# Pair sums on GpSimd and half-width Hadamard products in the last stage of a four-stage transformer kernel

## The reference, cut to what matters

```python
def act_quant(x, bits=8):
    qb = float(2 ** (bits - 1))
    scale = qb / jnp.clip(jnp.max(jnp.abs(x), axis=-1, keepdims=True), 1e-05)
    return jnp.clip(jnp.round(x * scale), -qb, qb - 1) / scale
def h_bitlinear(x, w):
    return jnp.einsum('bsh,oh->bso', act_quant(fwht(x)), weight_quant(w))
gate = bitlinear(x, w_gate)            # 1024 outputs
up = bitlinear(x, w_up)
x = x + h_bitlinear(jax.nn.silu(gate) * up, w_down)   # x is the layer norm's output inside
```

## Time and profile before

| | |
|---|---|
| median of 3 executions | 580.14 us (578.57 to 585.94) |
| the profiled execution | 581.71 us |
| its span, first to last instruction | 579.9 us |
| busy: TensorE, VectorE, ScalarE, GpSimd | 85%, 78%, 62%, 55% |

### The profile page before, as it was taken

How to read it: one execution, slowest core, us unless ns; L and a number is a source line. 1 busy time by engine, 2 the same in 40 slices (tenths; PEclk the granted TensorE clock), 3 DMA queues, 4 the chain that set the end, 5 groups by cost and what they waited for, 6 DMA issues and landing times.

```text
span 579.9 us, 11051 instructions
## 1 busy us (share of the span) xinstructions
PE 495.6 (85%) x3338; PEld 436.4 (75%) x3338; DVE 450.2 (78%) x1358; ACT 357.8 (62%) x903; POOL 318.6 (55%) x298
## 2 busy tenths in 40 slices
PE   0599979998889898995659999999899999588894
PEld 0478757877788887994449999999799998346673
DVE  4779967875877786756598889999989887769674
ACT  2345547253558676763237877878688889666643
POOL 2547671014467886415767788788577773363100
PEclk9989999999999998996597999999999999989997
DMA  8144454312364555545820000000000000000000
GB/s 276 38 126 129 131 152 126 90 58 67 98 195 111 188 187 161 144 131 145 284 62 19 28 21 19 29 19 1 2 1 2 2 1 2 0 1 9 11 28 27
DMA packets 27961, 45.24 MB, mean 78 GB/s; under 512 B 5697, under 2 KB 18849, under 8 KB 27265
## 3 DMA queue, kind: packets, MB, share of 16 engines
q1 hardware_dynamic: 21056, 28.15, 15.8%
q0 software_dynamic: 3792, 10.74, 7.2%
q10 hardware_dynamic: 3056, 5.65, 3.1%
HBM read 34.63 MB, written 8.85 MB: 75 GB/s over the span
## 4 chain that ended last, share of the span: by engine, by line
PE 48%; DVE 24%; issue 10%; DMA 7%; ACT 6%; POOL 5%; SPq 0%; DVEq 0%; ACTq 0%; POOLq 0%
PE bank L415 8%; PE bank L416 8%; PE bank L417 8%; PE bank L1080 8%; PE bank L1521 5%; DMA bw<-bits_dram 2%; DVE pT_lo L1580 2%; DVE sc L2081 1%; ACT pr L956 1%; PE bank L1476 1%; DVE X L1632 1%; DMA inb<-rows_kept,row_of 1%; DMA seg<-seg_dram 1%; DVE asel L1632 1%; PE bank L1282 1%
## 5 line engine op out<-in xcount | busy, mean ns | idle before, releaser
L584 POOL DMA_INDIRECT inb<-rows_kept,row_of x47 | 47.4, 1008 | 37.8 <-PE bank L1080 20.8
L956 ACT ACTIVATE pr<-sc,smin 128x256 f32<-128x256 f32 x128 | 63.3, 502 | 0.0
L661 POOL TENSOR_TENSOR Q_lo<-Q,Q_hi 128x512 fp32r<-128x512 f32 x32 | 41.5, 1297 | 22.7 <-ACT Q_hi L695 22.1
L2081 DVE CUSTOM_DVE_ANT_0 sc<-bank,bias 128x256 f32<-128x256 f32 x128 | 46.5, 418 | 0.1
L648 POOL TENSOR_TENSOR pr<-pr,srec 128x512 f32<-128x512 f32 x32 | 33.4, 1042 | 21.6 <-DVE srec L2088 21.6
L1580 DVE TENSOR_TENSOR pT_lo<-bank,pT_hi 128x512 fp32r<-128x512 f32 x64 | 41.1, 683 | 5.0 <-ACT pT_hi L695 5.0
L695 ACT ACTIVATE pT_hi<-bank 128x512 fp32r<-128x512 f32 x64 | 35.0, 595 | 13.6 <-PE bank L1080 13.3
L612 POOL DMA_INDIRECT yk<-slots_y,slot x32 | 33.7, 1052 | 14.0 <-issue 5.8
L655 POOL TENSOR_TENSOR Q<-Q,rot 128x512 f32<-128x512 f32 x32 | 41.2, 1286 | 0.0
L1080 PE MATMUL bank<-const,pr 128*128 128x128 f32 x256 | 34.8, 279 | 6.6 <-POOL pr L648 6.5
L965 ACT ACTIVATE pr<-pr,srec 128x256 f32<-128x256 f32 x64 | 29.1, 502 | 16.7 <-DVE srec L2088 16.7
(11 more groups left out here) (346 smaller groups left out, 1939.5 us busy)
## 6 DMA issues: line engine op xcount, KB each, us to landing
slots_y<-yb SPq DMA_DIRECT2D x47, 128.0 KB
wg_raw<-gate_up_dram SPq DMA_DIRECT2D x22, 256.0 KB, 2.8
bw<-bits_dram ACTq DMA_DIRECT2D x3, 1024.0 KB
wd_raw<-down_dram SPq DMA_DIRECT2D x16, 128.0 KB, 2.1
wo<-wo_dram SPq DMA_DIRECT2D x2, 1024.0 KB, 6.7
wd_raw<-down_dram SPq DMA_DIRECT2D x30, 64.0 KB, 2.2
gu_raw<-gate_up_dram SPq DMA_DIRECT2D x6, 256.0 KB, 3.5
X<-x_dram SPq DMA_DIRECT2D x2, 512.0 KB, 6.8
```

The source lines that it names most:

```text
L584: pool.indirect_dma_start(inb[:, j % NIN, :], None, rows_d, bass.IndirectOffsetOnAxis(row_of[:, j:j + 1], 0)).then_inc(slots_in[j % NIN], 16)
L661: pool.tensor_tensor(Q_lo[:, i % 2, :], Q[:, i % 2, :], Q_hi[:, i % 2, :].bitcast(F32), ALU.subtract).then_inc(queries_low_g, 1)
L956: e = act.activation(pr[:, i % 2, z, :], sc[:, i % 2, z, :], ACT.Exp, bias=smin[:, i % 2, z:z + 1], scale=-1.0, accum_out=ssum[:, i % 2, z ...
L2081: dve.tensor_tensor_reduce(sc[:, r, z, :], bank[2 + h][:, u * S:(u + 1) * S], bias[:, TB * b_ + u, :], 1.0, 3.0e38, ALU.add, ALU.min, smin ...
```

## The change

- GpSimd makes of two neighbouring units their sum and their difference (`pair`, tile `sd`), and high and low parts are taken of these, no longer of `hp`. The units' order of feature groups is changed to fit (`chunk`, `part_of`).
- The transform has one Hadamard level less to do: per tile 16 matmuls of 256 columns, each group pair going to its own half of a bank, with two by two signed copies in place of four by four.
- Transforms of tiles 4 and 6 use banks 2 and 3, those of 0 to 3, 5 and 7 banks 4 and 5.
- VectorE does `butterfly(t+1)` before `clip(t)`, and `x4(t-1)` at the end of step `t`. TensorE does `transform(t+1)` ahead of `turn_f(t-1)` from step 3 on.
- `feature_scale` has three small operations in place of four.

```diff
+            def pair(v, op):
+                if v >= 2:
+                    pool.wait_ge(bit_low_g, v - 1)
+                return pool.tensor_tensor(sd[:, v % 2, :], hp[:, 0, :], hp[:, 1, :], op).then_inc(pair_g, 1)
+            def lo_b(v):
+                pool.wait_ge(hidden_high_a, UNITS + v + 1)
+                n = v // NF
+                pool.tensor_tensor(hp_lo[n][:, part_of(v), :], sd[:, v % 2, :], hp_hi[n][:, part_of(v), :].bitcast(F32),
+                                   ALU.subtract).then_inc(bit_low_g, 1)
+            for v in range(0, 2 * NF, 2):
+                if v == BESIDE - 2:
+                    power3(NT - TB, TB)
+                pool.wait_ge(hidden_v, UNITS + v + 2)
+                pair(v, ALU.add)
+                pair(v + 1, ALU.subtract)
+                lo_b(v)
+                lo_b(v + 1)
...
             def hi_b(v):
-                act.wait_ge(hidden_v, UNITS + v + 1)
-                copy(hp_hi[n][:, c, :], hp[:, v % 2, :]).then_inc(hidden_high_a, 1)
+                act.wait_ge(pair_g, v + 1)
+                copy(hp_hi[v // NF][:, part_of(v), :], sd[:, v % 2, :]).then_inc(hidden_high_a, 1)
...
                 silu_b(v)
-                hi_b(v - 1)
+                hi_b(v - 2)
                 if v == LATE_TURN:
                     for t in range(NT - TB, NT):
                         bits_x(t)
+            hi_b(AHEAD - 2)
             hi_b(AHEAD - 1)
             f_copy(0)
...
+                for z in range(2):
+                    if w is not None:
+                        pe.wait_ge((butterfly_v, transform_copied_a)[z], (2 * (w + 1), w + 1)[z])
+                    for k in range(2):
+                        out = bank[transform_bank(t) + z][:, k * D:(k + 1) * D]
+                        for y, part in enumerate((hp_hi[n], hp_lo[n])):
+                            for r in range(2):
+                                e = pe.matmul(out, part[:, 4 * z + 2 * k + r, tile],
+                                              had[:, r, :, :].rearrange("p q j -> p (q j)"),
+                                              start=(y == 0 and r == 0), stop=(y == 1 and r == 1))
...
+            transform(3)
+            for t in range(3, NT + 2):
+                final(t - 2)
+                if t + 1 < NT:
+                    transform(t + 1)
+                if t <= NT:
+                    turn_f(t - 1)
...
                 if v >= 2:
-                    dve.wait_ge(bit_low_g, v - 1)
+                    dve.wait_ge(pair_g, v - v % 2)
                 dve.tensor_tensor(hp[:, v % 2, :], gsl[:, v % 2, :], bank[unit_bank(v, 1)][:, :], ALU.mult
...
+            butterfly(0)
+            for t in range(NT + 1):
                 if t < NT:
                     feature_scale(t)
                 for v in units_after(t):
                     gate_b(v)
+                if t + 1 < NT:
+                    butterfly(t + 1)
                 if t < NT:
                     clip(t)
                 for v in units_after(t):
                     up_b(v)
+                if t >= 1:
+                    x4(t - 1)
```

More of the change, by code:

```diff
@@ L237, in build @@
             m[k] for k in ("q_hi q_lo rot Q Q_hi Q_lo sc pr pT_hi pT_lo o_hi o_lo fqT hn2 sin2").split()]
-        xqT, invB, diag, gt, gsl, hp, had, f1, F = [m[k] for k in "xqT invB diag gt gsl hp had f1 F".split()]
+        xqT, invB, diag, gt, gsl, hp, had, sd, f1, F = [m[k] for k in "xqT invB diag gt gsl hp had sd f1 F".split()]
         hp_hi, hp_lo = [m["hpB_hi"], m["hpA_hi"]], [m["hpB_lo"], m["hpA_lo"]]
@@ L381, in x_bank, with chunk, part_of, transform_bank @@
             return t % 2 if t < NT - TB else 6 + t % 2
+        def chunk(v):
+            z, c0 = divmod(v % NF // 2, 2)
+            return 4 * z + 2 * (v % 2) + c0
+        def part_of(v):
+            z, c0 = divmod(v % NF // 2, 2)
+            return 4 * z + 2 * (v % 2) + c0
+        def transform_bank(t):
+            return 2 if t >= 4 and t % 2 == 0 else 4
+        def last_transform(t):
+            return max((w for w in range(t) if transform_bank(w) == transform_bank(t)), default=None)
         def final_bank(t):
@@ L984, in signs @@
                 act.wait_ge(masked_v, 4 * PAIRS)
-                for r in range(4):
-                    for q in range(4):
-                        e = act.activation(had[:, r, q, :], had1, ACT.Copy, scale=-1.0 if odd(r & q) else 1.0)
-                e.then_inc(signs_a, 1)
+                for r in range(2):
+                    for q in range(2):
+                        act.activation(had[:, r, q, :], had1, ACT.Copy, scale=-1.0 if r and q else 1.0)
             def bits_x(t):
@@ L1036, in f_copy @@
                     act.wait_ge(butterfly_v, 2 * (t - 1))
-                copy(f1[:, t % 2, :], bank[5][:, :]).then_inc(transform_copied_a, 1)
+                copy(f1[:, t % 2, :], bank[transform_bank(t) + 1][:, :]).then_inc(transform_copied_a, 1)
             def f_round(t):
@@ L1512, in transform @@
                 n, x = divmod(t, NT // 2)
-                tile = slice(x * P, (x + 1) * P)
-                for part, ready in ((hp_hi[n], hidden_high_a), (hp_lo[n], bit_low_g)):
-                    pe.wait_ge(ready, (UNITS if ready is hidden_high_a else 0) + NF * (n + 1))
-                    for z in range(2):
-                        if t >= 1 and ready is hidden_high_a:
-                            pe.wait_ge((butterfly_v, transform_copied_a)[z], (2 * t, t)[z])
-                        for r in range(4):
-                            m_ = had[:, r, :, :].rearrange("p q j -> p (q j)")
-                            e = pe.matmul(bank[4 + z][:, :], part[:, 4 * z + r, tile], m_,
-                                          start=(r == 0 and ready is hidden_high_a), stop=(r == 3 and ready is bit_low_g))
-                        if ready is bit_low_g:
-                            e.then_inc(transform_p, 1)
+                tile, w = slice(x * P, (x + 1) * P), last_transform(t)
+                pe.wait_ge(hidden_high_a, UNITS + NF * (n + 1))
+                pe.wait_ge(bit_low_g, NF * (n + 1))
+                if t == 4:
+                    pe.wait_ge(hidden_v, UNITS + 2 * NF)
+                for z in range(2):
[4 more added lines that the diff above has]
+                        for y, part in enumerate((hp_hi[n], hp_lo[n])):
+                            for r in range(2):
+                                e = pe.matmul(out, part[:, 4 * z + 2 * k + r, tile],
+                                              had[:, r, :, :].rearrange("p q j -> p (q j)"),
+                                              start=(y == 0 and r == 0), stop=(y == 1 and r == 1))
+                    e.then_inc(transform_p, 1)
             def turn_f(t):
@@ L1553, in _ @@
                 products(v)
-            pe.wait_ge(signs_a, 1)
             pe.wait_ge(xq_copied_a, 2 * NT)
-            for t in range(NT + 2):
-                if t < NT:
-                    transform(t)
+            for t in range(3):
+                transform(t)
                 if t >= 2:
                     final(t - 2)
-                for v in units_after(t)[:1]:
-                    products(v)
-                if 1 <= t <= NT:
+                products(AHEAD + 2 * t)
+                if t >= 1:
                     turn_f(t - 1)
-                for v in units_after(t)[1:]:
-                    products(v)
+                products(AHEAD + 2 * t + 1)
+            transform(3)
[5 more added lines that the diff above has]
+                    turn_f(t - 1)
         @block.vector
@@ L2253, in _ @@
             up_b(AHEAD - 1)
-            for t in range(NT + 2):
-                if t < NT:
-                    butterfly(t)
-                if t >= 2:
-                    x4(t - 2)
+            butterfly(0)
+            for t in range(NT + 1):
                 if t < NT:
```

28 lines of the change are left out of this document (11 added, 17 removed).

## The result

Four executions of the changed kernel have a median of **605.75 us** (604.54 to 608.4); four of the kernel before beside it 581.49 (578.57 to 585.94). The ratio is 1.040, with an interval from 1.036 to 1.045. The forecast was 608. The profiled execution took 606.64 us, its span 604.7.

A forecast was written before the change was run, and what follows sets the result against it. TensorE was half the chain; late tiles were bound by a 5.98 us loop of transform, copy and butterfly. Terms 9.1 + 15.9 - 0.4 + 3.3 = 27.9 us gave 609.6 profiled, 608 on the median, range 602 to 615.

The forecast's parts named there:

- R0: Start of tile 0's rounding; forecast at 532.6 in place of 523.5, 9.1 us later, with GpSimd setting the pace before the loop.
- R0 to R3: Early tiles, from tile 0's rounding to tile 3's: 37.8 us (11.1 + 11.1 + 15.6) against 21.9, 15.9 more.
- The third step: From tile 2's rounding to tile 3's: 15.6 us, waiting for four GpSimd operations, transform(4), half a turn and bits.
- R3 to R7: Late tiles, tile 3's rounding to tile 7's: four steps of 6.25 us, 25.0 against 25.4, set by VectorE and ScalarE.
- the TensorE loop worked out beforehand: Late tiles: half a turn, bits, final, transform and hand-overs, 4.95 us a tile, shorter than the 6.25 forecast.
- The clock: TensorE at the 1.2 GHz level after longer gaps, mainly at transform(0) and transform(4): 3.3 us added, bounded by 0 and 5.
- The sum: All forecast terms together: 27.9 us more, so the profiled execution would take 609.6 us in place of 581.7.
- the GpSimd operations come onto the chain: Early tiles: two GpSimd operations and a hand-over add 2.7 us per step, then high copy and bits 2.0; 11.1 against 6.56.
- even sums of no length: Early tiles: with sums taking no time a step would still be 6.4 + 2.0 us, over 6.56.
- hidden GpSimd work: Rival: sums hold up neither high copies nor bits, early steps bound by VectorE, late by TensorE; 573 us, chance 0.05.
- only this delay stays: Rival: only the 9.1 us delay before the loop remains, early steps overlapping somehow; 587 us, chance 0.08.
- A transform that stays slow in the late tiles: Rival: transform no cheaper, from 1.2 GHz or 256-column matmuls 0.24 apart; 612 to 616 us, chance 0.12.

The follow-up runs named there:

- short sums: Changed kernel with GpSimd's sums and differences over 8 of 512 columns from unit 2 on; 600.24 us, ratio 1.030.
- pairs alone: Kernel before with GpSimd sums and differences and half-width transforms, but old banks and old order of lists in the tile loop; 594.15 us, ratio 1.019.
- copy-first kernel: Changed kernel with ScalarE's copy for the next tile issued ahead of bits and rounding from tile 3 on; 599.59 us, ratio 1.028.
- the kernel with short sums and the new order of copies: Changed kernel with sums over 8 of 512 columns and ScalarE making a pair's two high copies together ahead of the loop; 596.93 us, ratio 1.024.

## Why the prediction was right

The direction, the engines and the places held, term by term:

- **R0, +9.1 forecast, +9.2 measured.** The first up of the second pair waited 2.04 us and the addition of attention's last tile moved from 499.70 to 501.48, as worked out. GpSimd then set the pace: its pairs came 4.91, 5.48 and 5.17 us apart, 15.6 in all, where three times 5.05 and 0.8 of delay were taken. Transform(0) did go at 1.2 GHz, and the copy waited 0.60 for it, where 0.8 was added. The agreement to 0.1 is partly luck, since R0 moves between 39.6 and 40.5 with the clock of transform(0).
- **R0 to R3, +15.9 forecast, +15.8 measured, partly by errors that cancel.** A step was put at 11.1 us and took 10.35: 6.06 us to the end of the second up in the rows above where 6.4 stood (silus, copy and butterfly overlap at their ends), 2.61 with the sums where 2.7 stood, 1.68 for high copy and bits where 2.0 stood. The third step was put at 15.6 at the full clock (its written terms add up to 15.5) and took 17.0, of which the low clock is 1.6 to 2.
- **R3 to R7, -0.4 forecast, -0.8 measured**: 6.14 a tile where 6.25 stood. The forecast set four even steps against 25.4 and did not say that before's first was 7.44; against the steady 5.98 the tile became longer, and the -0.8 comes from that first step, 1.3 us shorter. The chain was the one named, rounding to copy to butterfly to clip to reduce, and moving the copy out of it gave 4.80, near the TensorE loop worked out beforehand.
- **The clock, +3.3 forecast.** It showed where it was expected. The parts that can be read are 0.6 at transform(0), 1.6 to 2 at transform(4), and 0.6 behind R7, which I had not foreseen: the last turn took 1.97 us at the granted clock 0.50, before 1.35. Together 2.8 to 3.2. Left out, the sum would have been 24.6. The profiled spans differ by 24.8, and yet the trace shows the half clock on the path at all three places: the early steps, taken 1.5 too long, hid it. The Trainium skill (TensorE: Matmul & The Clock Gate, What's actually happening) puts the ramp under 1% of a typical kernel's span and lets a model leave it out. The trace agrees with the share, 2.8 to 3.2 of 604.7 us being 0.5%; it is over a tenth of this change's 24.8 all the same.
- **The sum** of 27.9 came out 3.1 too high against the spans, and the time 2.3 above the median.

The reading that did not hold is the reason given for the early tiles. The text let "the GpSimd operations come onto the chain" carry the steps. In the changed kernel they do lie on it, but what lengthened it is chiefly VectorE's butterfly ahead of the clip: 2.8 us of each of the first two steps and 3.3 of the third, shown by undoing that line, while the same sums in the old order cost 2.8 over the four steps to R4. The prediction's own remark that even sums of no length leave 6.4 + 2.0 us pointed there; measured with short sums were 8.88 and 9.89. Of the rivals, hidden GpSimd work (573) fails at the first term: R0 is late with either order (40.3 and 40.7). That only this delay stays (587) fails at the 15.8 behind it; it is nearer to pairs alone in the old order, 11.7 over before. A transform that stays slow in the late tiles was not seen: the granted clock of the tile shown is 1.00 and its matmuls start 0.12 apart.

The price of a sum, taken from the low parts at 1.27 us and bounded by VectorE's 0.68, was 1.269. The Trainium skill (GPSIMD Engine Reference, Engine selection) says about twice VectorE's time for such work; here 1269 against 681 ns is 1.86 times.

## What to carry to other kernels

An edit that pulls one operation ahead on one engine has to be priced by what it is pulled in front of: here the butterfly in front of the clip cost 2.8 to 3.3 us in each step whose units stand behind the clip, and nothing in the late steps once the copy stood ahead of the rounding (4.80 us with the butterfly still first). When the bounding engine is made cheaper, write down the next loop before counting the gain; a copy queued behind a rounding held back 5.7 us of it. Use a cheaper form that needs preparation only where the preparation is hidden and its gain is on the path, even if that is half of the work.

## What was unexpected of the hardware

- Work on TensorE up to 2.20 us before a transform did not save it from the 1.2 GHz level. The granted clock was still 1.00 in the two us from 564 on, where TensorE was busy 0.09, and 0.57 in the two behind them, busy 1.71: it fell as the transform began. With the work joined to the transform it stayed at 1.00.
- The same pause gave three clocks. Transform(0) stands behind 2.64 to 2.70 us without work in all of these: in the changed kernel it began at the granted clock 0.50, in the copy-first kernel it began at 1.00 and was at 0.50 from its middle on, and in the kernel with short sums and the new order of copies it kept 1.00. This moved R0 by up to 0.9 us between kernels whose lists are alike up to there.
- GpSimd and ScalarE waits that hide each other: removing either moved the start of transform(0) by 0.8 and 2.5 us, removing both by 5.3. A single experiment on the first would have called it a small matter.
- A sum over 8 columns on GpSimd took 0.20 us (the median of eight), one over 512 columns 1.27, so most of the time, though not all, is by length.
